# Transformer block on one core: the layer-normed input comes in already transposed from memory, and TensorE no longer transposes it

## The reference, cut to what matters

```
h  = layernorm(x)
xn = (h - mean(h)) * rsqrt(var(h) + eps) * ln_g + ln_b
q, k, v = split(xn @ W_qkv + b_qkv)
gate = sigmoid(h @ W_gate + b_gate); gate = gate / (mean(gate) + eps)
q = relu(q * gate)**2 + eps;  k = relu(k * gate)**2 + eps
# causal, per head: num_t = q_t . sum_{s<=t} k_s v_s^T ; den_t = q_t . sum_{s<=t} k_s + eps
x1 = x + (num / den) @ W_proj + b_proj
out = x1 + gelu(layernorm(x1) @ U1 @ V1 + b1) @ U2 @ V2 + b2
```

## Time and profile before

| | |
|---|---|
| median of 3 runs | 1833.25 us (1833.06 to 1835.95) |
| the profiled execution, its own time | 1834.25 us |
| its span in the trace | 1831.9 us |
| granted TensorE clock, mean | 0.995 |
| DVE, ACT, POOL busy | 1448.5, 683.9, 798.7 us |
| DMA, mean | 33 GB/s |

### The profile page before, as it was taken

One profiled execution on the slowest core, in us unless ns is written; L12 is line 12 of the kernel. 1 busy time (PEld: TensorE's weight loads), 2 busy tenths in 40 slices (PEclk: granted clock), 3 DMA queues, 4 the chain that ended last, 5 costly groups with the idle time before them and its releaser, 6 DMA issues.

```text
span 1831.9 us, 34348 instructions
## 1 busy us (share of the span) xinstructions
PE 1792.6 (98%) x13753; PEld 1539.9 (84%) x13753; DVE 1448.5 (79%) x2606; ACT 683.9 (37%) x1242; POOL 798.7 (44%) x1027
## 2 busy tenths in 40 slices
PE   7899999999999999999999999999999999999997
PEld 4688888888888888888888888888888888888876
DVE  7777878878878878878878788778887788787775
ACT  4233343343333333333333433333433433333332
POOL 3253444444444444435434444434444444444430
PEclk9999999999999999999999999999999999999999
DMA  6001000001010011010011010011010010100000
GB/s 216 26 13 35 29 31 31 24 29 36 24 35 24 24 36 36 24 36 25 24 36 36 24 36 24 25 35 35 25 36 24 24 36 25 35 24 27 28 18 24
DMA packets 34508, 61.06 MB, mean 33 GB/s; under 512 B 3672, under 2 KB 6256, under 8 KB 34352
## 3 DMA queue, kind: packets, MB, share of 16 engines
q1 hardware_dynamic: 33488, 57.31, 9.6%
q10 hardware_dynamic: 864, 1.57, 0.2%
HBM read 41.96 MB, written 16.91 MB: 32 GB/s over the span
## 4 chain that ended last, share of the span: by engine, by line
PE 93%; DVE 1%; POOL 0%; ACT 0%; issue 0%
PE ps_a L786 9%; PE ps_a L784 9%; PE ps_a L785 9%; PE ps_t L791 6%; PE ps_b L786 6%; PE ps_b L785 6%; PE ps_b L784 6%; PE ps_q L784 4%; PE ps_b L984 3%; PE ps_h L784 3%; PE ps_h L785 3%; PE ps_h L786 3%; PE ps_q L785 3%; PE ps_q L786 3%; PE ps_c L962 3%; PE ps_c L974 3%
## 5 line engine op out<-in xcount | busy, mean ns | idle before, releaser
L378 POOL TENSOR_TENSOR h_lo<-h_full,h_hi 128x512 fp32r<-128x512 f32 x244 | 313.8, 1286 | 500.7 <-DVE h_hi L604 500.7
L459 ACT ACTIVATE h_full<-ps_h,cols 128x256 f32<-128x256 f32 x512 | 211.1, 472 | 243.7 <-PE ps_h L786 236.0
L604 DVE CAST h_hi<-h_full 128x512 fp32r<-128x512 f32 x256 | 176.2, 688 | 98.0 <-ACT h_full L459 97.8
L784 PE MATMUL ps_b<-wx_hi,zt_hi 128*128 128x512 f32 x512 | 206.9, 404 | 5.3 <-DVE key_sums L714 3.1
L784 PE MATMUL ps_a<-wx_hi,zt_hi 128*128 128x512 f32 x512 | 208.2, 407 | 0.0
L786 PE MATMUL ps_b<-wx_hi,zt_lo 128*128 128x512 f32 x512 | 203.3, 397 | 0.0
L785 PE MATMUL ps_b<-wx_lo,zt_hi 128*128 128x512 f32 x512 | 203.2, 397 | 0.0
L786 PE MATMUL ps_a<-wx_hi,zt_lo 128*128 128x512 f32 x512 | 202.3, 395 | 0.0
L785 PE MATMUL ps_a<-wx_lo,zt_hi 128*128 128x512 f32 x512 | 201.8, 394 | 0.0
L340 POOL TENSOR_TENSOR small<-moments,eps_col 128x1 f32<-128x1 f32 x128 | 25.8, 201 | 391.5 <-DVE moments L753 327.1
L784 PE MATMUL ps_q<-h_hi,u_hi 128*128 128x256 f32 x512 | 159.5, 311 | 7.3 <-DVE h_lo L609 5.1
(11 more groups left out here) (173 smaller groups left out, 5053.0 us busy)
## 6 DMA issues: line engine op xcount, KB each, us to landing
xs<-L_attn_x SPq DMA_DIRECT2D x64, 256.0 KB, 2.8
out<-x1s SPq DMA_DIRECT2D x64, 256.0 KB, 2.1
key_sums<-carry_rows SPq DMA_DIRECT2D x60, 256.0 KB, 3.2
x1s<-L_attn_W_gate SPq DMA_DIRECT2D x4, 256.0 KB, 4.0
x1s<-L_ffn_U SPq DMA_DIRECT2D x4, 256.0 KB, 3.8
carry_rows<-key_sums SPq DMA_DIRECT2D x64, 2.0 KB
probs<-L_attn_W_qkv SPq DMA_DIRECT2D x3, 256.0 KB, 6.0
bias<-L_attn_b_qkv ACTq DMA_DIRECT2D x3, 256.0 KB, 6.8
```

The source lines that it names most:

```text
L378: E.tensor_tensor(h_lo[:, i % 2, :], h_full[:, i % 2, :], h_hi[:, i % 2, :].bitcast(F32), ALU.subtract).then_inc(s["h_lo_ready"], 1)
L459: last = E.activation(h_full[:, i % 2, a * GROUP:(a + 1) * GROUP], ps_h[i % 2][:, a * GROUP:(a + 1) * GROUP], ACT.Gelu_apprx_tanh, bias=b1 ...
L604: E.tensor_copy(h_hi[:, i % 2, :], h_full[:, i % 2, :]).then_inc(s["h_hi_ready"], 1)
L784: E.matmul(ps, wh, mh, start=start and i == 0, stop=False)
```

## The change

The host passes x a second time, as `x_turned`, with features on partitions (a host reshape, outside of the time). Per chunk:
- SP loads a chunk of it into `xt` (256 KB, `load_turned`), behind the load of `xs`. SP also turns the 128 row means from a column of `small` into a row that stands on all partitions: it writes the column to memory (`turned_rows`), waits, and reads it back broadcast into `rows` (`turn_rows`, at the head of a step, before the stores).
- GpSimd subtracts the means from `xt` in place (`center`), between its h_lo of pair 2 and that of pair 3. Its small products per chunk go from six to five.
- `z_head` (ScalarE) and `z_tail` (VectorE) read `xt` instead of `ps_t`, and both now stand behind their work on FFN pair 3. The values are deviations only; the first normalisation's scale is applied in the GATE evacuation (a `scalar_tensor_tensor` in place of a `tensor_tensor`), and the factors of the other three are changed to match.
- VectorE's `x_norm` and TensorE's `tz` are gone for chunks 1 to 63. Chunk 0 keeps them, without the scale.

The diff, cut to its core:

```
@@ SP
                 sp.dma_start(xs[:, c.slot, :], x[c.slot, bass.ds(c.row, P), :]).then_inc(x_in[c.slot], 16)
+                wait(sp, s["zt_ready"], Chunk(c.p, c.off - 2).done())
+                if c.p or c.off:
+                    load_turned(c)
+
+            def load_turned(c):
+                sp.dma_start(xt[:, c.half, :, :].rearrange(flat), x_turned[c.slot, c.row // P, :, :])\
+                    .then_inc(xt_in[c.slot], 16)
+
+            def turn_rows(c):
...
+                sp.wait_ge(s["x_stats"], c.done(2, 2))
+                sp.dma_start(rows_dram[c.slot, :].rearrange("(t a) -> t a", a=1), small[:, c.slot, 2:3]).then_inc(rows_out[c.slot], 16)
+                sp.wait_ge(rows_out[c.slot], c.turned())
+                wait(sp, s["z_ready"], Chunk(c.p, c.off - 2).done())
+                sp.dma_start(rows[:, c.half, :],
+                             rows_dram[c.slot, :].rearrange("(a t) -> a t", a=1).broadcast_to([P, P]))\
+                    .then_inc(rows_in[c.slot], 16)
...
             def step(p, b):
+                turn_rows(Chunk(p, b + 1))
@@ GpSimd
+            def center(c):
...
+                mine = xt[:, c.half, :, :]
+                pool.wait_ge(xt_in[c.slot], c.turned())
+                pool.wait_ge(rows_in[c.slot], c.turned())
+                E.tensor_tensor(mine, mine, rows[:, c.half, :].unsqueeze(1).broadcast_to([P, KT, P]),
+                                ALU.subtract).then_inc(s["z_ready"], 1)
...
                     h_tail(ffn, pairs[2])
+                center(Chunk(p, b + 1))
+                if ffn.exists and not is_last(p):
                     h_tail(ffn, pairs[3])
@@ ScalarE
+                    act.wait_ge(s["z_ready"], c.done())
+                    act.wait_ge(s["value_done"], before.done())
+                    turned = xt[:, c.half, :, :].rearrange(flat)
...
+                if ffn.exists:
+                    gelu(ffn, pairs[3])
                 z_head(Chunk(p, b + 1))
                 if ffn.exists:
-                    gelu(ffn, pairs[3])
@@ VectorE
+                    turned = xt[:, c.half, :, :].rearrange(flat) if c.p or c.off else ps_t[:, :]
+                    E.tensor_tensor(zt_lo[:, :, :].rearrange(flat), turned,
...
-                    E.tensor_tensor(gate[:, :], ps_b[:, :], bias[:, GATE, :], ALU.add)\
+                    dve.wait_ge(s["x_small"], n.done(5, 2))
+                    E.scalar_tensor_tensor(out=gate[:, :], in0=ps_b[:, :], scalar=small[:, n.slot, 1:2],
+                                           in1=bias[:, GATE, :], op0=ALU.mult, op1=ALU.add)\
...
-                x_norm(Chunk(p, b + 1))
...
-                z_tail(Chunk(p, b + 1))
                 if ffn.exists:
                     h_head(ffn, pairs[3], finishing)
+                z_tail(Chunk(p, b + 1))
...
-                    after = Chunk(p, b + 1)
-                    if after.exists:
-                        dve.wait_ge(s["tz_done"], after.done())
-                    elif d.exists:
+                    if d.exists:
@@ TensorE
-                tz(Chunk(p, b + 1))
                 if ffn.exists:
                     h_pair(ffn, pairs[3])
```

More of the change, by code:

```diff
@@ L142, in block_kernel @@
         xs = sb("xs", [P, 4, DM])
+        xt = sb("xt", [P, 2, KT, P])
+        rows = sb("rows", [P, 2, P])
         x1s = sb("x1s", [P, 4, DM])
@@ L152, in block_kernel @@
         vector_rows = gate[0:FT + 2 * KT, 0:P]
-        stats, moments = sb("stats", [P, 4, 6]), sb("moments", [P, 4, 2])
-        small = sb("small", [P, 4, 6])
+        stats, small = sb("stats", [P, 4, 6]), sb("small", [P, 4, 8])
         stats1, moments1 = sb("stats1", [P, 6]), sb("moments1", [P, 2])
@@ L201, in block_kernel @@
         x_in = [sem(f"x_in{i}") for i in range(4)]
+        xt_in = [sem(f"xt_in{i}") for i in range(4)]
+        rows_out = [sem(f"rows_out{i}") for i in range(4)]
+        rows_in = [sem(f"rows_in{i}") for i in range(4)]
         stored = [sem(f"stored{i}") for i in range(4)]
@@ L262, in load_x @@
                 sp.dma_start(xs[:, c.slot, :], x[c.slot, bass.ds(c.row, P), :]).then_inc(x_in[c.slot], 16)
+                wait(sp, s["zt_ready"], Chunk(c.p, c.off - 2).done())
[5 more added lines that the diff above has]
+            def turn_rows(c):
+                if not c.exists:
+                    return
+                sp.wait_ge(s["x_stats"], c.done(2, 2))
[5 more added lines that the diff above has]
+                    .then_inc(rows_in[c.slot], 16)
             def store(c):
@@ L346, in small_stats @@
                     return
-                var, r, done = moments[:, c.slot, 1:2], small[:, c.slot, :], s["x_small"]
+                var, r, done = small[:, c.slot, 3:4], small[:, c.slot, :], s["x_small"]
                 pool.wait_ge(s["x_stats"], c.done(2, 2))
@@ L351, in small_stats @@
                 tiny(r[:, 0:1], var, eps_col[:, :], ALU.add, done)
-                pool.wait_ge(done, c.done(6, 1))
+                pool.wait_ge(done, c.done(5, 1))
                 tiny(r[:, 1:2], r[:, 0:1], minus_half[:, :], ALU.pow, done)
[L354 to L361, removed]
+                tiny(r[:, 5:6], r[:, 0:1], eps_col[:, :], ALU.mult, done)
+                pool.wait_ge(done, c.done(5, 3))
+                tiny(r[:, 6:7], r[:, 5:6], var, ALU.add, done)
+                pool.wait_ge(done, c.done(5, 4))
+                tiny(r[:, 4:5], r[:, 6:7], minus_half[:, :], ALU.pow, done)
+            def center(c):
+                if not c.exists:
+                    return
+                mine = xt[:, c.half, :, :]
[3 more added lines that the diff above has]
+                                ALU.subtract).then_inc(s["z_ready"], 1)
             def add_bias(c):
                 if c.exists:
-                    pool.wait_ge(s["z_ready"], c.done())
+                    pool.wait_ge(s["x_stats"], c.done(2, 1))
+                    if not (c.p or c.off):
+                        pool.wait_ge(s["z_ready"], c.done())
                     E.tensor_tensor(xs[:, c.slot, :], xs[:, c.slot, :], bias_proj[:, :], ALU.add)\
@@ L428, in z_head @@
             def z_head(c):
-                if c.exists:
+                if not c.exists:
+                    return
+                before = Chunk(c.p, c.off - 1)
+                if before.exists:
+                    act.wait_ge(s["z_ready"], c.done())
+                    act.wait_ge(s["value_done"], before.done())
+                    turned = xt[:, c.half, :, :].rearrange(flat)
+                else:
                     act.wait_ge(s["tz_done"], c.done())
-                    E.activation(zt_hi[:, :, :].rearrange(flat), ps_t[:, :], ACT.Copy)\
-                        .then_inc(s["zt_hi_ready"], 1)
+                    turned = ps_t[:, :]
+                E.activation(zt_hi[:, :, :].rearrange(flat), turned, ACT.Copy).then_inc(s["zt_hi_ready"], 1)
             def tile_heads(ts):
@@ L523, in x_stats_wait @@
                     dve.wait_ge(x_in[c.slot], c.dmas())
-                    wait(dve, s["x_small"], Chunk(c.p, c.off - 4).done(6, 6))
+                    before = Chunk(c.p, c.off - 4)
+                    wait(dve, s["x_small"], before.done(5, 5))
+                    if before.exists:
+                        wait(dve, rows_out[c.slot], before.turned())
             def x_stats(c):
@@ L533, in x_moments @@
                 if c.exists:
-                    E.bn_aggr(moments[:, c.slot, :], stats[:, c.slot, :]).then_inc(s["x_stats"], 1)
+                    E.bn_aggr(small[:, c.slot, 2:4], stats[:, c.slot, :]).then_inc(s["x_stats"], 1)
             def x_norm(c):
[L538 to L544, removed]
+                E.tensor_scalar(zs[:, :], xs[:, c.slot, :], small[:, c.slot, 2:3], None, ALU.subtract)\
+                    .then_inc(s["z_ready"], 1)
             E.memset(state_bd[:, :, :, :].rearrange("p b k n -> p (b k n)"), 0.0).then_inc(s["state_zero"], 1)
@@ L810, in bias_products @@
                         .then_inc(s["stage_bias"], 1)
[L812 to L821, removed]
+            pe.wait_ge(s["z_ready"], 1)
+            transpose4(zs, s["tz_done"])
             def h_pair(g, i):
@@ L1036 @@
         args.append(nc.dram_tensor(name, a.shape, _mybir.dt.from_np(a.dtype), kind="ExternalInput").ap())
+    x = arrays["L0_attn_x"].reshape(BATCHES, POSITIONS, P, KT, P)
+    arrays["x_turned"] = _np.ascontiguousarray(x.transpose(0, 1, 4, 3, 2)).reshape(BATCHES, POSITIONS, P, DM)
+    args.append(nc.dram_tensor("x_turned", (BATCHES, POSITIONS, P, DM), _mybir.dt.float32, kind="ExternalInput").ap())
     out = nc.dram_tensor("out", (BATCHES, SEQ, DM), _mybir.dt.float32, kind="ExternalOutput").ap()
     carry_dram = nc.dram_tensor("carry_rows", (BATCHES, DM), _mybir.dt.float32, kind="Internal").ap()
-    block_kernel(nc, *args, out, carry_dram)
+    rows_dram = nc.dram_tensor("turned_rows", (BATCHES, P), _mybir.dt.float32, kind="Internal").ap()
+    block_kernel(nc, *args, out, carry_dram, rows_dram)
     r = _run(nc, [arrays], core_ids=[0])
```

14 lines of the change are left out of this document (8 added, 6 removed).

## The result

The changed kernel takes 1870.68 us (median, 1869.62 to 1872.32), the kernel before 1833.38 us beside it: a ratio of 1.0204 (95% interval 1.0191 to 1.0216), 37.3 us slower. The profiled execution took 1872.32 us over a span of 1870.6 us, 38.1 us more than the 1834.25 us of before, at the same granted clock of 0.995. The forecast was 1873 us, so the sign, the size and the place are to be compared.

A forecast was written before the change was run, and what follows sets the result against it. TensorE's queue was taken to bound the kernel; 30 pairs of steps at 0.96 + 0.51 - 0.13 = 1.34 us add 40.2 us to 1834.25, giving 1874.5, or 1873 us as median; range 1862 to 1886 (0.60), with rival A's low side 1848 to 1888.

The forecast's parts named there:

- TensorE is the bound, and only its queue and its waits count: Whole kernel: TensorE, busy 98% of the span, sets the time; only what leaves its queue and which waits enter count.
- Held behind GpSimd: VectorE's z_tail, now with two SBUF inputs, makes no progress until GpSimd's h_lo of pair 3 ends, finishing 0.55 us behind.
- The odd tail late by 1.44, the even one by 1.21: End of each step: VectorE's gate<-queries,key_sums ends 1.44 us late in odd steps, 1.21 us in even ones.
- `center` at 1.28: GpSimd's added subtraction of the means, 128x512, takes 1.28 us, with 1.04 as lower end and 0.3 more as upper.
- A stall of 0.96 in even steps at the keys' transposes: TensorE in each even step: the keys' transposes wait for x1t_lo and start about 957.26 instead of 956.30, 0.96 us.
- A stall of 0.51 in odd steps at the FFN's first product: TensorE in each odd step: the FFN's first product waits 0.51 us for the reader of the bank it reuses.
- TensorE's gain: At q_pair(2), the removed transposes' 0.41 us give 0 in odd steps and 0.13 us in even ones, limited by GpSimd's h_lo.
- The sum, 1.34 a pair: Steady steps: 0.96 + 0.51 - 0.13 = 1.34 us a pair, over 30 pairs +40.2 us.
- The start, counted at none, 0 to 1 allowed: Start of the kernel: 256 KB more load ahead of the last weight tiles; 0 to 1 us allowed, none counted.
- SP's queue: cost 0: SP's transfers of the means have 18 us in odd steps, some three fewer in even ones, and hold nothing: cost 0.
- rival E: SP's two transfers take over 15 us and hold center in every step: 1930 us and more; chance 0.04.
- Rival C: TensorE keeps the transposes' 0.41 us in 60 steps: 24.6 us faster, 1809 us; chance 0.07.

The follow-up runs named there:

- e4: Kernel before, with only the transposes of chunks 1 to 63 removed; z_head and z_tail read zs untransposed at their old places: 1833.13 us, 0.9999 of before.
- e1: Changed kernel, with z_tail reading the bank ps_t again instead of xt, everything else kept: 1837.25 us, 1.002 of before.
- e6: Kernel before, without the transposes of chunks 1 to 63 and with GpSimd's add_bias moved behind h_lo of pair 2: 1814.95 us, 0.9896 of before.
- e7: Changed kernel in full, with GpSimd's work reordered (center ahead of h_lo of pair 2) and z_head and z_tail moved: 1813.83 us, 0.9891 of before.

## Why the prediction was right, point by point

- *TensorE is the bound, and only its queue and its waits count.* Right. Taking 4 matmuls out of each step moved the time by nothing (e4).
- *Held behind GpSimd.* Right in place and size: `zt_lo` 1470 ns mean, ends 0.56 behind h_lo (0.55 forecast), h_hi 0.28 behind `center` (0.29). With one operand in a bank the same instruction takes 691 ns, and 33 us are gone (e1). The Trainium skill (SBUF — State Buffer, SBUF: two separate sides) has it that two such instructions exclude each other for the whole instruction. The trace agrees: 1470 ns against 691.
- *The odd tail late by 1.44, the even one by 1.21.* 1.40 and 1.17 to 1.21. *`center` at 1.28*: 1292 ns mean, the upper half of the bounds was the right choice.
- *A stall of 0.96 in even steps at the keys' transposes, released by `x1t_lo`.* 0.88: 0.82 at their start, and 0.06 more because a group that had to wait holds the queue for 0.41 and not 0.35.
- *A stall of 0.51 in odd steps at the FFN's first product.* 0.36. This term was mis-sized: the result of `x1s<-ps_c`, whose bank it reuses, ends at 949.53 + 0.68 = 950.21, 11.23 behind its GATE, where I had worked out 929.22 - 917.76 = 11.46; the product starts 0.14 behind it, not 0.05. About 0.11 of the first difference lies in GpSimd's small products: I took 0.27 for the one that is gone, and x1s came 0.38 earlier, since one of the five that are left no longer waits for the one ahead.
- *TensorE's gain: 0 in odd steps, 0.13 in even ones.* Odd: right, `h_pair(3)` starts 0.40 earlier than the shift (0.32 to -0.08), and `q_pair(2)`, which waits for h_lo, is back at +0.35. Even: `q_pair(2)` does gain 0.15, but by the key sums 0.10 of it is gone. The product that waits takes 0.81 us until the next where it took 0.71. What is left is 0.04. The step failed in that I priced a start and not the wait's own cost.
- *The sum, 1.34 a pair.* 1.19 measured; 30 pairs give 35.7 us and not 40.2. *The start, counted at none, 0 to 1 allowed*: 3.7 in the profiled executions, 1.6 to 2.4 with the end of the run by the medians. Pairs too dear by 4.5 and a start too cheap partly cancel, which is why 1873 against 1870.7 looks better than the terms were; that part is luck. For the start I asked what SP's loads delay, and not when the first `center` gets its rows and when it ends.
- *SP's queue: cost 0.* Right in the steady steps, and closer than I wrote; in the first step `center` does wait for the rows. The two transfers take 7.6 + 4.8 = 12.4 of the 18 us of room in odd steps (some 15 in even ones), not twice 3.2; rival E needed 15. The stores landed in 5.1 instead of 2.1 us without holding anyone.
- *Rival C*, the transposes' 0.41 us kept: e4 rules it out, and e6 shows its condition, h_lo of pair 2 earlier. Of the 24.6 us that it would give, 18.8 appear there. In e6's trace the way from the GATE of step 4 to that of step 63 is 20.9 us shorter than before (an odd step by 0.50, an even one by 0.21), and the GATE of step 4 is 2.9 us later; why it is later is open.

## What to carry to other kernels

Work that leaves the bounding engine is worth nothing while the next instruction on it waits for another engine's result: look first for who delivers it, and move that first. An operand moved from a bank to SBUF can make an instruction collide with another engine, as here VectorE's with GpSimd's. Its price is then the end of the neighbour's product and not its own duration; place it where the neighbour is idle or nearly through (e7: the same change in another order, 57 us less). When every term is sized in the steady state, price the first steps as well, and compare more than one trace of them.

## What I had not expected of the hardware

In these traces a product that had to wait costs TensorE more than the wait: 0.81 us against 0.71 from `q_pair(2)` to the key sums, and 0.41 against 0.35 for four transposes. A column of 0.5 KB, 4 bytes from each partition, lands in 7.6 us, more than twice the 3.1 us of a 256 KB tile. With two more 256 KB loads early on SP's queue (issued at 6.95 and 11.93 in the changed kernel), a 256 KB load on ScalarE's queue landed in 7.6 to 10.5 us in five traces; in the five traces of kernels without `x_turned` it took 6.1 to 7.3.
